# Smaller pieces in which spilled rows and the last matrix's weights are loaded, in a graph-convolution kernel

## The chip, the cores and the metric

One Trainium2 chip, one core of it. The metric is the device time of one launch in microseconds. A core has a matrix engine (TensorE, PE in the profile), a vector engine (VectorE, DVE), a scalar engine (ScalarE, ACT), GpSimd (POOL), a queue processor SP that issues DMAs, and 16 DMA engines that carry them.

## The reference

A graph of 6250 service nodes with 200,000 random edges goes through two graph convolutions of width 32. Then 512 requests, each a user and three services, are looked up, laid side by side (128 features) and multiplied by a 128 x 6250 matrix.

```python
def gcn_conv(x, W, b, src, dst, n):
    h = x @ W
    s, d = concatenate([src, arange(n)]), concatenate([dst, arange(n)])
    deg = segment_sum(ones, d, n);  dis = rsqrt(deg)
    msgs = h[s] * (dis[s] * dis[d])[:, None]
    return segment_sum(msgs, d, n) + b
g = relu(gcn_conv(service_emb, W1, b1, src, dst, 6250))
g = gcn_conv(g, W2, b2, src, dst, 6250)
x = concatenate([user_emb[user_idx], g[context_idx].reshape(512, 96)], axis=1)
return x @ fc_W + fc_b            # 512 x 6250, float32
```

## The kernel before

The sum over edges is made a dense product. The nodes are cut into 49 chunks of 128, and the 49 chunks of destinations into 14 groups (`SIZES`): one of 1 chunk, two of 2 chunks, eleven of 4. The adjacency of a group is a table of small counts in fp8, one 128 x 128 tile for each source chunk and destination chunk: 196 tiles for a group of four chunks, 25,088 bytes in each of the 128 partitions.

Up to about 330 us the edges are sorted. From there to 593 us the groups are built one after the other: TensorE makes the tiles out of one-hot rows (L1431), ScalarE evicts them into one of three slots, and TensorE at once uses them for the first layer (L1449, tile `psY`). Since three slots don't hold 14 groups, SP writes each of the first 11 to DRAM (`spill`, L573).

Then comes the second layer, in the order `ORDER`: the last three groups, which still lie in their slots, and then groups 10, 9, ... down to 0, which are read back. Five slots are in use now, `place2[i]` for the i-th group. Four programs run side by side:

- TensorE (from L1493) waits for `loaded` of the group's slot and runs 49 matmuls of 96 columns for each chunk, each with a weight load of its own (L1449, tile `pp`), then raises `y2_done`.
- SP (from L592) issues the reloads in the same order. The loads of the groups at places 3 and 4 wait only for TensorE's last tile of the building stage (`filled`); those at place i from 5 on wait for `y2_done` of i - 4, which says that group i - 5 has left the slot. After the reloads SP loads the last matrix (`load_fc`): its weights once `y2_done` is 10, its bias, spread over all partitions, once it is 11. Both count on `fc_in`.
- VectorE sums the three parts of a group (L1221) and scales them (L1223, L1213).
- ScalarE's queue writes the result to a table in DRAM (L803): 128 bytes for each node, 64 KB for a group of four chunks.

When all table rows are in DRAM, GpSimd gathers the requests' rows (L677), TensorE turns them into features (L1530, L1535), waits for all of `fc_in`, and multiplies by the last matrix in blocks of 512 columns (L1550). VectorE adds the bias, and the result leaves on the queues of SP and ScalarE.

The reload splits each group in four (`LOAD_PARTS`), so a DMA moves 6272, 3136 or 1600 bytes of each partition for a group of 4, 2 or 1 chunks. The last matrix goes in pieces of `FC_PART` = 1568 columns of four bytes; its weights take two DMAs a piece (96 and 32 partitions), its bias one.

Of the kernel before, what the change touches and what calls it, by code (L numbers as in the profile page):

```python
# [92 lines left out]
SPILL_PARTS = 4  # L93
RUN_UP = (8, 12, 36)
AHEAD_OF = {1: 12, 3: 6}
LOAD_PARTS = 4
FC_PART = 1568


UNIT = 2.0 ** -9  # L100
# [36 lines left out]
def chunks_of(g):  # L137
    return SIZES[g]


def first_chunk(g):
    return sum(SIZES[1:g]) if g else sum(SIZES[1:])
# [6 lines left out]
def group_of(b):  # L149
    return next((g for g in range(1, NG) if b < first_chunk(g) + SIZES[g]), 0)  # L150
# [13 lines left out]
def tiles_of(g):  # L164
    return NH * chunks_of(g)


def bytes_of(g):
    return -(-tiles_of(g) // 2) * 2 * P


def pairs_of(g):
    return -(-tiles_of(g) // PAIR)


def first_half(g):
# [23 lines left out]
def pairs_before(g):  # L200
    return sum(pairs_of(k) for k in range(g))


def gcn_kernel(nc, user_idx, context_idx, edge_index, user_emb, service_emb,
# [13 lines left out]
    with ctx:  # L218
        def sem(name):
            return ctx.enter_context(nc.semaphore(name))  # L220
# [72 lines left out]
        def at(offset, size, dt):  # L293
            return arena[:, offset:offset + size].bitcast(dt)
# [123 lines left out]
        loaded = [sem(f"loaded{k}") for k in range(5)]  # L418
# [73 lines left out]
        for k, counted_then in enumerate(tiles_by):  # L492
            needed = sum(c0 < counted_then for _, c0, _ in begun)
            assert units_ready(TURN_STAGES[k] - 1, k) >= UNITS * needed and words_ready_by(TURN_STAGES[k], k) >= WORDS * needed
# [6 lines left out]
        ORDER = list(range(NG - SLOTS, NG)) + list(range(NG - SLOTS - 1, -1, -1))  # L501
        KEPT = [g % SLOTS for g in ORDER[:SLOTS]] + [3, 4]
        place2 = [KEPT[i % 5] for i in range(NG)]
        NSPILL = NG - 3

        def adj_tile(slot, n):
            return adj8[slot][:, n // 2, :, n % 2]

# [19 lines left out]
        def _(sp):  # L528
# [39 lines left out]
            for g in range(NSPILL):  # L568
                for k in range(SPILL_PARTS):
                    a, b = (pairs_of(g) * n // SPILL_PARTS for n in (k, k + 1))  # L570
                    c, e = (min(n * PAIR // 2 * 2 * P, bytes_of(g)) for n in (a, b))
                    sp.wait_ge(evicted, pairs_before(g) + b)
                    sp.dma_start(spill[g, :, c:e], at(adj_at[g % SLOTS] + c, e - c, U8)).then_inc(spilled[g % SLOTS], 16)  # L573
# [5 lines left out]
            def load_fc(slot, what):  # L579
                tile = at(adj_at[slot], N * 4, F32)  # L580
                whole = fc_W if what == 0 else fc_b[None, :].to_broadcast((P, N))
                for c in range(0, N, FC_PART):
                    w = min(FC_PART, N - c)
                    if what == 0:
                        sp.dma_start(tile[0:CTX * D, c:c + w], whole[D:P, c:c + w]).then_inc(fc_in, 16)
                        sp.dma_start(tile[CTX * D:P, c:c + w], whole[0:D, c:c + w]).then_inc(fc_in, 16)
                    else:
                        sp.dma_start(tile[:, c:c + w], whole[:, c:c + w]).then_inc(fc_in, 16)

            with sp.If(is_bad == 0):  # L590
                sp.wait_ge(filled, pairs_before(NG))
                for i in range(3, NG):  # L592
                    if i >= 5:
                        sp.wait_ge(y2_done, i - 4)
                    part = -(-bytes_of(ORDER[i]) // LOAD_PARTS)
                    for c in range(0, LOAD_PARTS * part, part):
                        w = min(part, bytes_of(ORDER[i]) - c)
                        sp.dma_start(at(adj_at[place2[i]] + c, w, U8), spill[ORDER[i], :, c:c + w]).then_inc(loaded[place2[i]], 16)
                for k in range(2):
                    sp.wait_ge(y2_done, NG - 4 + k)  # L600
                    load_fc(place2[(NG + k) % 5], k)
# [79 lines left out]
        def _(act):  # L681
# [97 lines left out]
            for g in range(NG):  # L779
                if g >= SLOTS:  # L780
                    act.wait_ge(spilled[g % SLOTS], 16 * SPILL_PARTS * (g // SLOTS))
                    act.wait_ge(y_done, g - SLOTS + 1)
                if g == 2:
                    act.wait_ge(flags_set, 3)
                for k in range(pairs_of(g)):
                    gp = pairs_before(g) + k
                    n0, n1 = k * PAIR, min((k + 1) * PAIR, tiles_of(g))
                    m0, m1 = n0 // 2, -(-n1 // 2)
                    act.wait_ge(filled, gp + 1)
                    nc.scalar.mul(adj16[g % SLOTS][:, m0 * P:m1 * P], bank(gp)[:, 0:(m1 - m0) * P], PAIR_SCALE).then_inc(evicted, 1)  # L790
                    if g and k == LAG - 1:
                        set_y(g - 1)
                    if g + 2 < NG and k in relative_at(g):
                        relative(g + 2, relative_at(g).index(k))
# [24 lines left out]
        def _(dve):  # L819
# [184 lines left out]
            def on_stage(step, cur, stages, turns):  # L1004
                histogram(units_ready(stages, turns))
                if stages in GLUE_AT:
                    for part in GLUE_AT[stages]:
                        glue(part)
                _, level, bit, mirror, domain = step
                s, t = keys[cur], keys[1 - cur]  # L1010
                dve.wait_ge(sorted_to, stages + 1)
# [275 lines left out]
            def mix_features(b):  # L1287

                dve.wait_ge(feat_mixed, b + 1)
                V.tensor_scalar(featT[0:CTX * D, b * P:(b + 1) * P], psX[0:CTX * D, b % 2 * P:(b % 2 + 1) * P], bias2[:, 0:1], None, ALU.add).then_inc(feat_ready, 1)  # L1290
            copy_features(0)
            mix_features(0)
            dve.wait_ge(fc_in, 48 * -(-N // FC_PART))
            n = 0
# [15 lines left out]
        def _(pe):  # L1310
# [136 lines left out]
            def spread(tile, layer, slot, n, c):  # L1447
                b, dd = divmod(n, c)
                return MM(tile[:, dd * D3:(dd + 1) * D3], adj_tile(slot, n), features(layer, b), start=(n == 0), stop=(n == NH * c - 1))  # L1449
# [4 lines left out]
            def run_up(n, tile=pp[1][:, BANK:2 * BANK]):  # L1454

                for _ in range(n):
                    MM(tile[:, 0:P], ident[:], above[:], start=True, stop=True)
# [27 lines left out]
            g = NG - 1  # L1485
# [6 lines left out]
            with pe.If(is_bad == 0):  # L1492
                for i, g in enumerate(ORDER):  # L1493
                    c = chunks_of(g)
                    tile = pp[i % 3]
                    if i >= 3:
                        pe.wait_ge(y2_read, i - 2)
                        pe.wait_ge(loaded[place2[i]], 16 * LOAD_PARTS * (i // 5 + (1 if i % 5 >= 3 else 0)))
                    for b in range(NH):
                        if i == 0 and b == first_chunk(group_of(b)):  # L1500
                            pe.wait_ge(x_done, group_of(b) + 1)
                        for dd in range(c):
                            ins = spread(tile, 1, place2[i], b * c + dd, c)
                    ins.then_inc(y2_done, 1)
                run_up(RUN_UP[2])
# [26 lines left out]
            def weigh_features(b):  # L1532

                pe.wait_ge(feat_copied, b + 1)
                MM(psX[0:CTX * D, b % 2 * P:(b % 2 + 1) * P], W2b[:], featT[0:CTX * D, b * P:(b + 1) * P], start=True, stop=True).then_inc(feat_mixed, 1)  # L1535
            pe.wait_ge(users_in, 16 * BB)
            turn_features(0)
            weigh_features(0)
            pe.wait_ge(fc_in, 48 * -(-N // FC_PART))
            n = 0  # L1540
# [33 lines left out]
```

## Time and profile before

| | us |
|---|---|
| median of three runs | 767.07 (767.07 to 769.0) |
| the profiled execution | 769.29 |
| its span | 767.5 |

The span is measured between the first and the last instruction of the profiled execution; its own time contains the little that lies around it. In the profile, queue q1 is that of SP, q10 that of ScalarE, q0 that of GpSimd, and q8 carries instructions. The granted clock is a share of TensorE's full 2.4 GHz. "issue" in the chain of waits is time in which an engine waited for nothing that the profile shows. The share of a DMA queue is the time its packets took, as a share of 16 engines' time; it can pass 100% in a short stretch, as a packet is counted whole where it starts. A stretch can be asked for by itself; its rows are then those of packets and issues that start in it.

### The profile page before, as it was taken

What the parts mean: (1) busy time and instruction counts of PE and PEld (TensorE: products, weight loads), DVE (VectorE), ACT (ScalarE), POOL (GpSimd) and SP (SyncE); (2) the same over time, 40 slices, a digit from 0 to 9 for tenths busy, and PEclk for the clock granted to TensorE, in tenths of its full rate; (3) what the DMA queues carried; (4) which work ended last, traced back from release to release, by engine and by line L of the source; (5) the groups of instructions that cost most, each with busy time, mean ns of one, the idle gap of its engine ahead of it and who ended that gap; (6) DMA issues with size and microseconds to landing.
All of it is one profiled execution on the core that took longest, in us unless ns stands there. A gap on an engine that the chain in (4) does not pass through costs nothing.

```text
span 767.5 us, 21867 instructions
## 1 busy us (share of the span) xinstructions
PE 600.2 (78%) x9504; PEld 563.7 (73%) x9504; DVE 600.4 (78%) x1436; ACT 423.3 (55%) x770; POOL 178.6 (23%) x181
## 2 busy tenths in 40 slices
PE   0453657747657755578699999999999999998897
PEld 0343657747657854478699999999999999998543
DVE  9999999999999999786999999999982211111386
ACT  4996188889879311357588888888877000000000
POOL 1100000020000000577766666666100000000500
PEclk9967779799778875589899999999999999999999
DMA  7000000000000000245366665556000999859376
GB/s 128 2 1 1 1 1 1 1 5 2 1 4 1 2 0 1 72 112 177 120 204 210 210 200 196 193 207 210 13 3 23 417 415 399 286 132 274 90 306 284
DMA packets 39143, 94.13 MB, mean 123 GB/s; under 512 B 19097, under 2 KB 21843, under 8 KB 39044
## 3 DMA queue, kind: packets, MB, share of 16 engines
q1 hardware_dynamic: 24340, 74.28, 26.3%
q0 software_dynamic: 5216, 9.91, 6.0%
q10 hardware_dynamic: 9488, 8.52, 3.5%
q8 instruction: 76, 1.25, 0.7%
q14 instruction: 23, 0.19, 0.1%
HBM read 48.50 MB, written 44.18 MB: 121 GB/s over the span
## 4 chain that ended last, share of the span: by engine, by line
PE 52%; DVE 37%; issue 3%; ACT 3%; POOL 2%; DMA 2%; SPq 0%; DVEq 0%; POOLq 0%
PE pp L1431 17%; PE pp L1449 14%; PE psY L1449 13%; DVE arena L962 12%; DVE arena L963 12%; PE pp L1550 6%; DVE arena L949 3%; POOL arena L656 2%; ACT arena L713 2%; PE pp L1367 1%; DMA arena<-ordered_keys,window 1%; DVE arena L957 1%; DVE arena L958 1%; PE psX L1418 1%; DVE arena L960 1%
## 5 line engine op out<-in xcount | busy, mean ns | idle before, releaser
L656 POOL DMA_INDIRECT arena<-ordered_keys,window x147 | 157.3, 1070 | 217.9 <-DMA ordered_keys<-arena 147.5
L790 ACT ACTIVATE arena<-pp 128x512 uint16<-128x512 f32 x308 | 172.0, 584 | 43.5 <-PE pp L1431 41.2
L1431 PE MATMUL pp<-arena 128*128 128x128 fp8e4 (+1 forms) x2401 | 189.4, 221 | 7.7 <-DVE arena L1141 7.7
L713 ACT ACTIVATE arena<-arena,neg_word 128x780 fp8e4<-128x780 bf16 (+1 forms) x200 | 170.1, 945 | 0.0
L1431 PEld LDWEIGHTS pp<-arena 128*128 128x128 fp8e4 (+1 forms) x2401 | 148.3, 98 | 8.2 <-issue 6.2
L1449 PE MATMUL psY<-arena 128*128 128x96 bf16 x2401 | 150.6, 207 | 2.7 <-ACT y_s L774 2.6
L1449 PEld LDWEIGHTS psY<-arena 128*128 128x128 fp8e4 x2401 | 123.4, 98 | 2.9 <-ACT arena L790 2.7
L1140 DVE TENSOR_SCALAR arena<-arena 128x384 int32<-128x384 int32 (+5 forms) x224 | 111.0, 496 | 7.4 <-PE pp L1431 7.3
L1449 PE MATMUL pp<-arena 128*128 128x96 bf16 x2401 | 105.8, 207 | 8.2 <-issue 8.2
L1449 PEld LDWEIGHTS pp<-arena 128*128 128x128 fp8e4 x2401 | 104.3, 99 | 9.8 <-issue 9.7
L962 DVE TENSOR_TENSOR arena<-arena 128x832 f32<-128x832 f32 (+4 forms) x121 | 107.5, 888 | 3.9 <-ACT arena L736 1.1
L963 DVE TENSOR_TENSOR arena<-arena 128x832 f32<-128x832 f32 (+4 forms) x121 | 106.9, 884 | 0.0
L1347 PE MATMUL psY<-arena 128*128 128x128 fp8e4 x1024 | 74.7, 242 | 25.6 <-DVE arena L949 21.1
L1347 PEld LDWEIGHTS psY<-arena 128*128 128x128 fp8e4 x1024 | 74.1, 143 | 27.0 <-issue 14.4
L1367 PE MATMUL pp<-ident,arena 128*128 128x128 f32 x202 | 39.6, 373 | 57.2 <-DVE arena L963 57.1
L1221 DVE TENSOR_REDUCE arena<-pp 128x128 f32<-128x384 f32 (+2 forms) x14 | 7.1, 508 | 95.2 <-PE pp L1449 95.2
L1367 PEld LDWEIGHTS pp<-ident,arena 128*128 128x128 f32 x202 | 34.3, 197 | 59.8 <-DVE arena L963 59.8
L1141 DVE TENSOR_SCALAR arena<-arena 128x384 int32<-128x384 int32 (+5 forms) x224 | 73.1, 327 | 0.0
L766 ACT ACTIVATE arena<-arena,neg_low 128x128 f32<-128x128 f32 x147 | 47.9, 391 | 16.9 <-DMA arena<-ordered_keys,window 16.8
L677 POOL DMA_INDIRECT feat<-context_table,ccl x12 | 11.3, 943 | 174.8 <-DMA context_table<-arena 171.4
L1550 PE MATMUL pp<-arena 128*128 128x512 f32 (+1 forms) x104 | 44.8, 586 | 0.5 <-DVE arena L1290 0.5
L1347 PE MATMUL pp<-arena 128*128 128x128 fp8e4 x539 | 39.4, 242 | 6.5 <-ACT arena L713 6.5
(205 smaller groups left out, 518.8 us busy)
## 6 DMA issues: line engine op xcount, KB each, us to landing
arena<-adjacency_spill SPq DMA_DIRECT2D x32, 784.0 KB, 10.5
adjacency_spill<-arena SPq DMA_DIRECT2D x24, 768.0 KB, 4.0
adjacency_spill<-arena SPq DMA_DIRECT2D x8, 832.0 KB, 4.0
out_dram<-arena SPq DMA_DIRECT2D x12, 512.0 KB, 2.6
out_dram<-arena ACTq DMA_DIRECT2D x8, 512.0 KB, 2.9
arena<-adjacency_spill SPq DMA_DIRECT2D x8, 392.0 KB, 4.8
arena<-ordered_keys,window POOLq DMA_INDIRECT x147
arena<-in_L_rec_fc_b_dram SPq DMA_DIRECT2D x3, 784.0 KB, 12.2
```

Source lines behind the costliest of these rows:

```text
L656: nc.gpsimd.indirect_dma_start(gath[:, k, q, :], None, ordered, bass.IndirectOffsetOnAxis(ap=window[:, q, d:d + 1], axis=0)).then_inc(gat[ ...
L713: ins = nc.scalar.activation(cols8[n % BUFS][:, 4 * u:4 * u + 4, 0:c1 - c0], high4[:, :, c0:c1], ACT.Sign, bias=neg_word[:, u:u + 1], satu ...
L790: nc.scalar.mul(adj16[g % SLOTS][:, m0 * P:m1 * P], bank(gp)[:, 0:(m1 - m0) * P], PAIR_SCALE).then_inc(evicted, 1)
L962: V.tensor_tensor(o_low, low, high, ALU.min)
L963: return V.tensor_tensor(o_high, low, high, ALU.max)
L1140: V.tensor_scalar(src32[h][:, i, :, 0:b - a], bit32[:, 0:4, a:b].bitcast(I32), abs(BIT - i), BITS, shift, ALU.bitwise_and)
L1141: ins = V.tensor_scalar(dst32[h][:, i, :, 0:b - a], bit32[:, 4:8, a:b].bitcast(I32), abs(BIT - i), BITS, shift, ALU.bitwise_and)
L1347: ins = MM(counts_of(s), cols8[n % BUFS][:, :, i], rows8[n % BUFS][:, :, i, :], start=False, stop=False)
L1367: ins = nc.tensor.transpose(ps[q][:, b * P:(b + 1) * P], src[:, c + b * P:c + (b + 1) * P], ident[:])
L1431: ins = MM(bank(gp)[:, (n - n0) // 2 * P:((n - n0) // 2 + 1) * P], src_hot(h, n - a), dst_hot(h, n - a), start=n % 2 == 0, stop=n % 2 == 1 ...
L1449: return MM(tile[:, dd * D3:(dd + 1) * D3], adj_tile(slot, n), features(layer, b), start=(n == 0), stop=(n == NH * c - 1))
L1550: MM(bank(n)[:, 0:w], featT[:, b * P:(b + 1) * P], fcW[:, c:c + w], start=True, stop=True).then_inc(fc_mm, 1)
```

## The change

The number of pieces of a reload now goes with the group's chunks: `loads_of(g)` is 4 for each chunk, so 16, 8 or 4 DMAs for a group, of 1568 bytes a partition (1600 for the group of one chunk, whose 49 tiles are rounded up to 50). What TensorE waits for is counted by `loads_to`, which sums the loads that went to the slot so far. `FC_PART` goes from 1568 to 784 columns, so the weights take 16 DMAs and the bias 8.

```diff
-LOAD_PARTS = 4
-FC_PART = 1568
+LOADS_A_CHUNK = 4
+FC_PART = 784
...
+def loads_of(g):
+    return LOADS_A_CHUNK * chunks_of(g)
...
+        def loads_to(i):
+
+            return sum(loads_of(ORDER[k]) for k in range(3, i + 1) if k % 5 == i % 5)
...
-                    part = -(-bytes_of(ORDER[i]) // LOAD_PARTS)
-                    for c in range(0, LOAD_PARTS * part, part):
+                    part = -(-bytes_of(ORDER[i]) // loads_of(ORDER[i]))
+                    for c in range(0, loads_of(ORDER[i]) * part, part):
...
-                        pe.wait_ge(loaded[place2[i]], 16 * LOAD_PARTS * (i // 5 + (1 if i % 5 >= 3 else 0)))
+                        pe.wait_ge(loaded[place2[i]], 16 * loads_to(i))
```

SP's queue before, from the branch after the building stage (L590) on: the reloads (L598, partitions x bytes), the weights of the last matrix (L585 and L586, partitions x columns), and its bias (L588).

```order
L590 COMPARE_AND_BRANCH
L598 DMA arena<-adjacency_spill 128x6272 x32
L598 DMA arena<-adjacency_spill 128x3136 x8
L598 DMA arena<-adjacency_spill 128x1600 x4
L585 DMA arena<-in_L_rec_fc_W_dram 96x1568
L586 DMA arena<-in_L_rec_fc_W_dram 32x1568
```

The same place of SP's queue in the changed kernel, whose lines are 8 further down:

```order
L598 COMPARE_AND_BRANCH
L606 DMA arena<-adjacency_spill 128x1568 x144
L606 DMA arena<-adjacency_spill 128x1600 x4
L593 DMA arena<-in_L_rec_fc_W_dram 96x784
L594 DMA arena<-in_L_rec_fc_W_dram 32x784
```

44 reloads have become 148, with the last group's four as they were, and each pair of weight DMAs holds half the columns (there are eight pairs now, and were four). No instruction has moved past another on any engine.

## Rows read from the trace of the kernel before

**Rows 1.** The page of the kernel before, its header.

```profile
span 767.5 us, 21867 instructions
```

**Rows 2.** Chain that ended last, 592.2 to 720 us: start us, length us, what.

```profile
593.46 0.32 issue
...
606.65 0.61 issue
607.26 5.60 PE pp L1449 x128
612.86 0.60 issue
...
672.53 0.61 issue
673.14 21.88 PE pp L1449 x511
695.02 2.42 issue
697.44 7.17 PE pp L1449 x127
704.62 0.21 issue
...
708.34 2.62 DMA context_table<-arena
...
718.49 2.16 PE pp L1550 x3
```

**Rows 3.** Waits, 590 to 720 us: total us, times, longest us.

```profile
PE pp L1449 <- issue: 8.2, 13, 2.4
```

**Rows 4.** DMA, 597 to 657: queues (packets, MB, share); issues (KB, us to landing).

```profile
q1 hardware_dynamic: 4317, 24.08, 97.6%
...
q8 instruction: 10, 0.16, 1.0%
...
context_table<-arena ACTq DMA_DIRECT2D x6, 64.0 KB, 12.0
```

**Rows 5.** DMA, 610.9 to 611.0 us.

```profile
q8 instruction: 1, 0.02, 61.2%
```

**Rows 6.** DMA, 670.7 to 670.9 us.

```profile
q8 instruction: 1, 0.02, 29.6%
```

**Rows 7.** DMA, 674.2 to 674.4 us.

```profile
q8 instruction: 1, 0.02, 31.7%
```

**Rows 8.** DMA, 680.0 to 680.2 us.

```profile
q8 instruction: 1, 0.02, 28.8%
```

**Rows 9.** DMA, 694.4 to 694.6 us.

```profile
q8 instruction: 1, 0.02, 43.9%
```

**Rows 10.** Windows: stretch, PE, PEld, DVE, ACT, POOL busy; then granted clock, DMA share, GB/s.

```profile
698.80:702.20 3.40, 3.40 (x48) 3.40 (x44) 0.81 (x3) 0.00 (x0) 0.00 (x0) 0.50 1.04 339
```

**Rows 11.** DMA, 677.4 to 678.4 us.

```profile
q1 hardware_dynamic: 247, 0.35, 97.6%
```

**Rows 12.** DMA, 675.8 to 682 us.

```profile
q1 hardware_dynamic: 572, 0.81, 45.1%
...
context_table<-arena ACTq DMA_DIRECT2D x1, 64.0 KB, 5.7
```

**Rows 13.** Timeline of SP's queue, 592 to 600 us: start us, us, what.

```profile
592.30 4.21 SPq L598 DMA_DIRECT2D arena<-adjacency_spill  x8
```

**Rows 14.** Timeline of SP's queue, from 684 us.

```profile
684.21 0.35 SPq L585 DMA_DIRECT2D arena<-in_L_rec_fc_W_dram  x1
...
692.54 1.77 SPq L588 DMA_DIRECT2D arena<-in_L_rec_fc_b_dram  x4
```

**Rows 15.** DMA, whole span: the last piece of the bias.

```profile
arena<-in_L_rec_fc_b_dram SPq DMA_DIRECT2D x1, 773.0 KB, 16.6
```

**Rows 16.** DMA, 667.1 to 670.7 us, an issue of this stretch.

```profile
context_table<-arena ACTq DMA_DIRECT2D x1, 64.0 KB, 6.8
```

## The prediction

> **What bounds the kernel now.** I read the page's header first [rows 1]: the execution spans 767.5 us; its own time is 769.29, the median of three runs 767.07. The change touches only loads that SP issues after 592 us, so next I read the chain that ended last from there [rows 2]. From 593.8 to 707.5 us it is TensorE's second layer, one matmul row after another, cut by pieces called "issue": 0.61 us at 606.65, then one behind nearly every 128 matmuls (that is 256 instructions, each matmul has its weight load), 0.61 at 672.53, then 2.42 at 695.02 and 0.21 at 704.62. The waits by engine add all of them to 8.2 us in 13 stops [rows 3]. The stops come by count of instructions and not at a group's start (196 matmuls), where TensorE would wait for a load: no load is late.
>
> The DMA view says what they are. From 597 to 657 us SP's queue keeps the 16 engines busy for 97.6% of the time, and beside it q8 carries 10 packets of instructions of about 16 KB each (0.16 MB), as many as TensorE uses blocks of 256 instructions [rows 4]. The block that began at 607.26 had its successor's packet start at 610.9, 3.6 us later [rows 2, 5]; TensorE ran dry at 612.86 and went on at 613.46, 2.5 us after that start. So a packet that starts within 5.60 - 2.5 = 3.1 us of the block costs nothing, and a later one costs the excess. Four more starts: 3.8 us after the block that began at 672.53 - 5.60 = 666.93, under pieces of 3136 bytes [rows 6]; 1.1 us after 673.14, with the engines idle [rows 7]; 1.4 us after 673.14 + 5.47 = 678.61 (5.47 is a quarter of the four blocks in 21.88), under pieces of 1600 bytes [rows 8]; 4.9 us after 673.14 + 3 x 5.47 = 689.55, under the weights of the last matrix [rows 9]. The start at 4.9 us made the 2.42 us stop, and behind it the granted clock was 0.50 (the 1.2 GHz level) for 3.4 us [rows 10]: the next 128 matmuls took 7.17 us and not 5.60 [rows 2].
>
> **The change, part by part.** The reload goes from 44 DMAs to 8 x 16 + 2 x 8 + 4 = 148; rows of 6272 or 3136 bytes become 1568 (1600 in the last group). The last matrix takes 16 DMAs and its bias 8, where they took 8 and 4, with rows of 3136 bytes. Same bytes, same gates, same order.
>
> *Stops under the reload.* They are 8.2 - 0.32 (the branch at 593.46) - 2.42 - 0.21 = 5.25 us. What stands in front of an instruction packet? Over the idle start of 1.1 us the 6272-byte stretch adds 2.5 us. A packet there takes 0.245 us on an engine (24.08 MB in 0.976 x 16 x 60 us is 25.7 bytes a ns), so about 10 packets. If the number of packets in front is what stays, 10 to 16 of them at 0.07 us add 0.7 to 1.1 us: the start is at 1.8 to 2.2 us, under 3.1, and all 5.25 us go. If the bytes in front stay (10 x 6272 = 63 KB, 40 small packets, 2.8 us), the start is at 3.9 and the stops stay. For the first speaks rows 8, 1.4 us under nearly the pieces that the change wants; against it that this load was only four DMAs long and nearly drained, and rows 6, where pieces of half the size gained nothing (3.8 us). I take 5.25 gone, zero as the other end.
> The Trainium skill ("DMA: Bandwidth & Descriptors", section "Queues, rings and completion order") says that an engine drains a whole packet, typically 9 to 17 descriptors, from one queue before it turns to the next. The 10 worked out for 6272 bytes agree with it, the 3136-byte start does not (2.7 us of packets half as long would be some 20); by it the stops go, by a count of bytes they would stay.
>
> *Stops under the last matrix.* 2.42 + 0.21 us of stop and 7.17 - 5.60 = 1.57 us of slow clock: 4.2 us. The packets there become half as long, not a quarter, and rows 6 show 3136 bytes still late. Bounds 0 and 4.2; I take half, 2.1 us.
>
> *Are the loads still in time?* A group of 4 chunks is needed every 196 x 43.75 ns = 8.6 us (5.60 us for 128). In the best microsecond of the 1600-byte load 0.35 MB moved at 97.6% [rows 11], 22.4 bytes a ns, 70 ns for 1568 bytes; over the whole short load 0.81 MB at 45.1% of 6.2 us [rows 12] gives 18.1 bytes a ns, 87 ns. All reloads are 148 x 8 = 1184 packets for each engine, plus some 5 us of table rows and semaphores. From 592.8 at 70 ns they end at 681; the group that is needed last of the full ones, the eighth, is there by 668 and wanted at 593.8 + 10 x 8.6 = 679.5. SP issued its first eight in 4.21 us, 0.53 each [rows 13]: 16 take 8.4 us, inside 8.6. It is late by the first two groups' 32 issues (17 us against a gate at 602), and hardly catches up, but slots are loaded some 20 us ahead. I take the cost as 0; the cover is this lead.
>
> *The last matrix's loads.* Issued at 684.21, bias at 692.54 [rows 14], its last piece landing 16.6 us after its issue [rows 15], the last of four in 1.77 us and so at 693.9: at 710.5: 26.3 us in all. TensorE wants them at 718.49 [rows 2], 8.0 us later. Now the gate opens 5.25 us earlier (679) and the need comes 7.35 - 2.4 = 4.95 us earlier (713.5). With 681 as start of the data and 1 us for shorter rows they land near 707: hidden, 6 us spare.
>
> *The last table write, late instead.* It took 2.62 us, its queue just drained [rows 2]. TensorE now ends at 700, while the bias loads run to 706, and a write beside them is slow: 12.0 us for 64 KB beside 6272-byte packets [rows 4], 6.8 beside 3136 [rows 16], 5.7 beside 1600 [rows 12]. For this last one of 16 KB beside 3136-byte packets I bound 2.6 and 6.8 us and take 5.0: 2.4 us lost (0 to 4.2). The gather and the features wait for it.
>
> Sum: -5.25 - 2.1 + 2.4 = -4.95 us. The profiled execution would come to 764.3; set on the median, 767.07 - 4.95 = **762.1 us**. Own range: 759.0 to 765.5.
>
> **The rivals.**
> *Bytes in front, not packets.* The stops stay at 0.4 to 0.8 us. Since the smaller packets keep the engines full to 681 and not 672, one or two more blocks (at 673 and 678) meet a stop: +1. Time 767.5 (766 to 769). For it: rows 6. Against it: rows 8.
> *The loads become the bound (the other side).* Its place is the reload. The last matrix's data must begin by 713.5 - 25.3 = 688 to be in time; 1184 packets and 5 us must fit in 95 us, so it decides from 76 ns a packet, or 0.65 us for an issue of SP. At 87 ns [rows 12] the eighth full group ends at 592.8 + 8 x (128 x 0.087 + 0.4) = 685 against 679.5, and all reloads at 701; weights and bias follow to 726, features wait for them and not for the table, and the time is 718.5 to about 726: +7, 774 us. Against it: the 87 ns contain the slow first packets and the tail of a four-DMA load, and rows 11 show 70; in its favour, nothing here shows a long stretch of such packets, and 76 lies between.
> The Trainium skill (same page, section "Bandwidth") asks for DMAs of at least 1 MiB, with about 2.0 us of fixed cost each. Taken one behind the other, 148 DMAs of 200 KB at an estimated 2.46 us would be 364 us. The trace denies that they go one behind the other: four of 200 KB were all down in 6.2 us at most [rows 12].
> *Everything gains.* All stops and the slow clock go, 9.4 us, and the table write loses 0 to 2 because the weights, too, run ahead: 758.5. For it: 1.57 us hang on one stop alone. Against it: rows 6.
>
> **How the numbers follow.** Forecast 0.46; bytes in front 0.20; loads the bound 0.20; everything gains 0.10; mixtures, 0.04. A change of 0.3% (2.3 us) is what a measurement can tell. Faster: 0.46 x 0.95 + 0.10 + a tenth of the second and third = 0.58; the second rival gives most of the 0.20 for the same, the third most of the 0.22 for slower. Range 757.5 to 772.5: it leaves out about 0.15 of the slow case and 0.03 below.
>
> **What would show it.** In the chain of the changed kernel: no "issue" every 128 matmuls between 594 and 680; TensorE's 1965 matmuls there unbroken and the gate of the last matrix at about 679. q8's packets start within 3 us of a block. The reload's last packet near 681 (at 688 or later the slow rival begins). The last table write 5 us long. One stop of about 1 us between 680 and 700, and perhaps no stretch at 0.50 clock. It is wrong if stops stay at 0.6 us, or if a stop stands at the start of a group and not by count: that would be a late load.

## The result and the profile after

The changed kernel takes 763.0 us in the median of 20 runs (759.55 to 769.0), the kernel before 767.07 (761.98 to 770.12, 20 runs). The ratio is 0.9954, 95% interval 0.9937 to 0.9972: 0.5% faster, 4.1 us between the medians. Single runs of either kernel spread over 8 to 10 us, so the traces below are compared from the second layer's own entry, its first matmul.

The header and the chain that ended last of the changed kernel, from 585 us (start us, length us, what); both answers, since the long piece hides where the layer begins:

```profile
span 758.4 us, 21983 instructions
```

```profile
590.61 0.30 issue
590.91 3.10 PE pp L1457 x69
```

```profile
591.97 98.64 PE pp L1457 x2321
690.61 1.76 issue
692.37 2.68 PE pp L1457 x59
...
695.89 4.17 DMA context_table<-arena
...
703.38 3.21 DMA feat<-context_table,ccl
...
708.82 9.43 PE pp L1558 x16
```

Its waits from 590 to 720 us (total us, times, longest us), to be held against [rows 3]:

```profile
PE pp L1457 <- issue: 2.1, 2, 1.8
```

The stops under the reload (ten of 0.33 to 0.82 us in the kernel before, 5.25 us in all) are gone; of [rows 2] only the branch and one stop of 1.76 us under the last matrix's weights are left, and no slow clock follows it in this trace. Windows of the layer (stretch, PE, PEld, DVE, ACT, POOL busy, granted clock, DMA share, GB/s):

```profile
590.90:674.40 83.50, 83.49 (x1965) 83.50 (x1966) 13.30 (x37) 0.22 (x1) 0.00 (x0) 1.00 1.04 356
674.40:684.10 9.70, 9.70 (x233) 9.70 (x230) 2.28 (x6) 0.00 (x0) 0.00 (x0) 1.00 1.05 287
684.10:692.40 8.30, 6.54 (x155) 6.43 (x152) 0.81 (x3) 0.00 (x0) 0.00 (x0) 1.00 1.05 294
```

The DMA view of 597 to 657 us answers to [rows 4] (queue: packets, MB, share of 16 engines; issues: KB, us to landing):

```profile
q1 hardware_dynamic: 15129, 21.09, 99.1%
...
q8 instruction: 11, 0.18, 1.1%
...
arena<-adjacency_spill SPq DMA_DIRECT2D x106, 196.0 KB, 4.0
context_table<-arena ACTq DMA_DIRECT2D x7, 64.0 KB, 5.3
```

The reload moves 21.1 MB where it moved 24.1, at full engines, and a table write beside it lands in 5.3 us and not 12.0. A reload DMA lands 4.0 us after its issue. SP issues without a pause (timeline of its queue from 591 us, start and length in us; the first three of the 148 reload DMAs were issued before, from 589.45 us on):

```profile
590.76 83.21 SPq L606 DMA_DIRECT2D arena<-adjacency_spill  x145
674.40 0.35 SPq L593 DMA_DIRECT2D arena<-in_L_rec_fc_W_dram  x1
```

That is 0.574 us for each 200 KB, or 350 GB/s, about what the engines move: the load queue never gets long. The bytes of all DMAs issued so far, less those of the packets begun, are what stands in the queue. Counted so every six microseconds from 596 to 674 us, 25 to 45 rows an engine are waiting (40 to 70 KB); in the kernel before, from 596 to 656 us, they swung between 7 and 47 rows of 6272 bytes (45 to 296 KB).

The two kernels from the layer's first matmul (us after it). Each row is one profiled execution, and the changed kernel's two are 3.5 us apart at the end, so differences of 2 to 3 us mean little:

| kernel | entry at | layer ends | table landed | last matrix starts | span ends |
|---|---|---|---|---|---|
| before | 593.8 | 113.7 | 117.2 | 124.7 | 173.7 |
| changed | 590.9 | 104.1 | 109.2 | 117.9 | 167.5 |
| changed, again | 597.3 | 106.0 | 109.2 | 116.7 | 164.0 |

Of the 9.1 us between the first two spans, 2.9 are the entry, which the change doesn't touch; 9.6 are gained in the layer, 2.8 given back between layer and last matrix, 0.6 in the last matrix. In the second trace of the changed kernel the layer gains 7.7. Its stop under the weights is followed by a slow clock, as in the kernel before (59 matmuls in 4.25 us and not 2.68; granted clock 0.60 from 699.0 to 703.3 us, so mostly the 1.2 GHz level):

```profile
696.97 2.04 issue
699.01 4.25 PE pp L1457 x59
```

The last matrix differs only in its first 16 matmuls, by the clock: 8.80 us before (granted 0.81), 9.43 in the first trace (0.75), 7.10 in the second (1.00). TensorE had waited 1.2, 3.6 and 0.9 us for the gathered features just before.

### The profile page after: what moved, and what is told of

It reads as the page before. It is cut to its first block, busy times and chain, and to the rows that moved or that the text cites. A ratio compares the mean times of both kernels' runs of the same rounds, so it can differ in the third digit from the quotient of the medians.

```text
span 758.4 us, 21983 instructions
## 1 busy us (share of the span) xinstructions
PE 591.7 (78%) x9504; PEld 555.6 (73%) x9504; DVE 600.8 (79%) x1436; ACT 423.1 (56%) x770; POOL 179.4 (24%) x181
## 4 chain that ended last, share of the span: by engine, by line
PE 53%; DVE 37%; ACT 3%; issue 2%; POOL 2%; DMA 2%; SPq 0%; DVEq 0%; POOLq 0%
PE pp L1439 17%; PE pp L1457 13%; PE psY L1457 13%; DVE arena L970 13%; DVE arena L971 12%; PE pp L1558 6%; DVE arena L957 3%; POOL arena L664 2%; ACT arena L721 2%; PE pp L1375 1%; DVE arena L965 1%; DMA arena<-ordered_keys,window 1%; DVE arena L966 1%; PE psX L1426 1%; DVE arena L968 1%
## 5 line engine op out<-in xcount | busy, mean ns | idle before, releaser
L1457 PE MATMUL pp<-arena 128*128 128x96 bf16 x2401 | 102.4, 206 | 2.1 <-issue 2.1
L1457 PEld LDWEIGHTS pp<-arena 128*128 128x128 fp8e4 x2401 | 102.1, 98 | 2.3 <-issue 2.3
L1355 PEld LDWEIGHTS psY<-arena 128*128 128x128 fp8e4 x1024 | 73.9, 143 | 26.1 <-issue 13.8
L1314 DVE TENSOR_TENSOR arena<-pp,arena 128x512 f32<-128x512 f32 (+1 forms) x52 | 33.9, 658 | 11.2 <-PE pp L1558 10.6
```

What stands on the lines that cost most here:

```text
L1355: ins = MM(counts_of(s), cols8[n % BUFS][:, :, i], rows8[n % BUFS][:, :, i, :], start=False, stop=False)
```

## The experiments

In three of them the last matrix is as before (1568 columns), in the others as in the changed kernel, unless said. Ratios are to the kernel before, timed on the same chip.

**The reload alone.**

```diff
-FC_PART = 784
+FC_PART = 1568
```

> The reload in 1568-byte rows, the last matrix in pieces of 1568 columns as before. If the packets in front of an instruction packet count (theory P), the ten stops of 0.3 to 0.8 us under the reload go (5 us) and the stop of about 2.4 us with its slow clock under the weights stays: second layer about 108 us long instead of 113.7, time 1 to 4 us under before. If the whole gain came from the last matrix's pieces, this run equals before.

Ratio 0.9939 (0.9909 to 0.997). Its chain:

```profile
593.73 94.31 PE pp L1457 x2215
688.04 1.92 issue
689.96 5.57 PE pp L1457 x127
695.53 2.63 issue
698.16 4.23 PE pp L1457 x59
...
703.22 2.39 DMA context_table<-arena
```

The layer is 108.7 us long, as expected, and the whole measured gain is here, though it ends 4.6 us later than the changed kernel's first trace: by its end no load is waiting in the queue any more, and the table write is short.

**The last matrix alone.**

```diff
-    return LOADS_A_CHUNK * chunks_of(g)
+    return LOADS_A_CHUNK
```

> The reload in four pieces a group as before, the last matrix in pieces of 784 columns. Theory P: about ten stops under the reload, 5 us, stay; the stop under the weights falls from 2.4 to 1 to 2 us without a slow clock. Second layer about 111 to 112 us, time 0 to 3 us under before. If the last table write loses 1.5 to 3 us beside the shorter rows, that eats it: no change.

Ratio 1.0006 (0.9982 to 1.003), no change. Stops under the reload 0.23 to 0.61 us each, nine of them, one of 1.66 under the weights and no slow clock: the layer ends after 109.1 us, 4.6 before the old one, but the last matrix starts only 3.7 earlier and the span ends 2.7 earlier in this trace (its first 16 matmuls take 9.85 us, at a granted clock of 0.72); the median shows none of it.

**Wide rows in small DMAs.**

```diff
-                        sp.dma_start(at(adj_at[place2[i]] + c, w, U8), spill[ORDER[i], :, c:c + w])...
+                        for p in range(0, P, 32):
+                            sp.dma_start(at(adj_at[place2[i]] + c, w, U8)[p:p + 32, :], spill[ORDER[i], p:p + 32, c:c + w])...
```

> As many and as large DMAs as the changed kernel (148 of 200 KB), but each of 32 partitions with rows of 6272 bytes (6400 in the last group), two packets an engine. Theory P (what stands in front are packets, each as long as its row): rows of 6272 bytes bring the stops of 0.4 to 0.8 us back, 4 to 6 us in all, although the DMAs are small. Rival D (small DMAs let the instruction packets through): no stops under the reload, as in the changed kernel.

Ratio 1.0511 (1.0462 to 1.056). Stops came back, and far larger. Chain, and the reload in the DMA view of 597 to 657 us:

```profile
605.79 2.86 issue
608.65 6.94 PE pp L1458 x128
615.59 1.73 issue
617.32 5.60 PE pp L1458 x128
622.92 3.07 issue
```

```profile
q1 hardware_dynamic: 3417, 14.30, 98.7%
...
arena<-adjacency_spill SPq DMA_DIRECT2D x92, 196.0 KB, 21.3
```

The instruction packet of the block at 617.32 starts at 623.1, 5.8 us in. So small DMAs alone don't let the instruction packets through. It isn't clean, though: DMAs of 32 partitions also move only 14.3 MB in the 60 us, 15 bytes a ns and engine, which alone makes anything in front of an instruction packet last longer. SP, which issues faster than that, has 150 to 336 KB an engine waiting from 608 us on.

**Rows of 3136 bytes.**

```diff
-LOADS_A_CHUNK = 4
+LOADS_A_CHUNK = 2
```

> Rows of 3136 bytes throughout the reload (2 DMAs a chunk). Theory P with 10 to 16 packets in front at 0.124 to 0.142 us: instruction packets start 2.3 to 3.4 us into a block: no stops or a few under 0.3 us, under 1 us in all. Rival B (a fixed number of bytes in front): starts at 3.6 us or later and ten stops, 4 to 5 us in all; but B already fails on the changed kernel's starts at 0.8 to 2.4 us, so a threshold in the row's length between 1568 and 3136 would be its last refuge.

Ratio 1.0029 (1.0005 to 1.0054). Ten stops of 0.33 to 0.60 us under the reload. Packets are half as long, and the instruction packets start where they did. This was the first sign against the prediction's count of packets. In the block that begins at 605.72 the packet comes 3.5 us in (DMA view, 609.2 to 609.4 us):

```profile
q8 instruction: 1, 0.02, 27.5%
```

**Rows of 12544 bytes.**

```diff
-    return LOADS_A_CHUNK * chunks_of(g)
+    return 2
```

> Two DMAs a group, rows of 12544 bytes, the last matrix in pieces of 784 columns. Theory C, formed from the runs so far: an instruction packet waits for what already stands in the load queue of its engine, but for no more than some 90 KB of it, whatever the rows' length. It expects starts 3.5 to 4 us into a block, stops of 0.3 to 0.9 us, as with rows of 6272 bytes. Theory P, the prediction's (some 10 to 16 rows in front, each as long as its bytes): 10 rows of 0.47 us, starts 5 us or more into a block and stops of 2 us and more.

One execution, 768.23 us. Nine stops of 0.17 to 0.72 us under the reload: no worse than at 6272 bytes. A packet here lasts 0.48 us; ten of them would have made stops of nearly 3 us. In the block that begins at 607.13 the instruction packet starts 3.5 us in.

**Short rows, deep queue.** The decisive one: the rows of the changed kernel in the DMAs of the old one.

```diff
+                    part = bytes_of(g) // (4 * n)
+                    to = at(adj_at[place2[i]], bytes_of(g), U8).rearrange("p (n k w) -> p k n w", k=4, w=part)
+                    of = spill[g, :, 0:bytes_of(g)].rearrange("p (n k w) -> p k n w", k=4, w=part)
+                    for k in range(4):
+                        sp.dma_start(to[:, k], of[:, k]).then_inc(loaded[place2[i]], 16)
```

> Rows of 1568 bytes as in the changed kernel, but four of them from each partition in one DMA: 44 DMAs of up to 784 KB as before, so SP runs ahead and the queue is as deep in bytes as before. The last matrix in pieces of 1568 columns. Theory C: with 90 KB in front of an instruction packet (57 rows, 3.8 us) the stops of 0.3 to 0.8 us come back although the rows are short. Theory P (10 to 35 rows in front): starts at 1 to 2.5 us, no stops under the reload, second layer as with the 1568-byte reload alone (108.7 us).

Ratio 1.0018 (0.9994 to 1.0043): no gain left. Its waits from 590 to 720 us, its chain, the DMA view of 611.1 to 611.2 us, and that of 597 to 657 us:

```profile
PE pp L1459 <- issue: 9.5, 14, 2.4
```

```profile
607.27 0.30 issue
607.58 5.60 PE pp L1459 x128
613.18 0.33 issue
...
619.11 0.60 issue
```

```profile
q8 instruction: 1, 0.02, 59.7%
```

```profile
q1 hardware_dynamic: 14787, 22.48, 101.5%
...
arena<-adjacency_spill SPq DMA_DIRECT2D x28, 784.0 KB, 11.7
```

As many packets of the load queue as in the changed kernel (14787 against 15129), but a DMA lands 11.7 us after its issue and not 4.0, the instruction packet starts 3.5 us into its block, and the stops are all back. So short rows alone don't free the instruction packets, and a count of packets in front doesn't describe them: the same rows without the long queue (the reload alone) had no stop.

Put together, a start less the idle start of 1.1 us [rows 7], times the engines' rate, is an estimate of what was in front: 2.5 us at 25.7 bytes a ns are 64 KB with rows of 6272; 2.4 at 24.8 are 60 KB with 3136; 2.4 at 26.0 are 62 KB with 12544; 2.4 at 23.1 are 55 KB here; and 4.7 at 15.1 are 71 KB in the wide rows of small DMAs. In packets the same are 10, 19, 5, 35 and 11. Nor is it one DMA of the load queue: one holds 50, 25, 100, 50 and 12.5 KB an engine. The idle start isn't always the same (0.4 us after 684.02 us in the kernel before), so these are good to some 20 KB.

Counted over all traces, TensorE's blocks split by what stood in the load queue when they began. In each of the 46 blocks with 100 KB or more an engine (DMAs over 128 partitions, rows of 1568 to 12544 bytes) the instruction packet started 3.4 to 3.9 us in, and a stop followed. With 60 to 75 KB it started 1.0 to 2.5 us in under rows of 1568 and 1600 bytes (21 blocks), and 2.5 to 4.0 us in under longer ones (10 blocks). A short queue and short rows go together in the changed kernel; how much the rows add when the queue is short, no run here separates.

**Wide rows, paced.**

```diff
+                        if len(sent) >= DEPTH:      # DEPTH = 2
+                            sp.wait_ge(sent[-DEPTH], 16 * sent.count(sent[-DEPTH]))
```

> DMAs and rows of before (6272 bytes, last matrix in pieces of 1568 columns), but SP issues a reload only when the one before the last has landed: at most two are out, 16 rows an engine. Theory C: the queue in front is mostly one DMA or less (8 rows, 2 us) and never the full 16 for long: starts at 1.5 to 3.2 us, at most a few stops under 0.3 us. Theory P: rows of 6272 bytes, at least 8 to 10 in front as long as the engines are busy: stops stay. The loads themselves come a little later, never late for a group.

Ratio 1.0269 (1.0228 to 1.031). In the timeline of TensorE the first 1066 matmuls run unbroken, where the old kernel had six stops. Then three stops by count of instructions come back (0.25, 0.44 and 0.63 us), and from 654 us on the loads are late (waits, 590 to 722 us):

```profile
593.99 45.47 PE L1464 MATMUL pp<-arena 128*128 128x96 bf16 x1066 [0.29 <-issue]
639.71 5.57 PE L1464 MATMUL pp<-arena 128*128 128x96 bf16 x127 [0.25 <-issue]
645.72 5.60 PE L1464 MATMUL pp<-arena 128*128 128x96 bf16 x128 [0.44 <-issue]
```

```profile
PE pp L1464 <- DMA arena<-adjacency_spill: 15.0, 5, 4.5
```

A DMA lands 6.3 us after its issue, so two at a time move 1.6 MB in 6.3 us, 255 GB/s. The expectation "never late" was wrong. In the six blocks from 601.3 to 633.9 us, at whose start 21 to 60 KB an engine were waiting, the instruction packets started 0.8 to 2.5 us in; in the three blocks after them, with 52 to 73 KB, 3.5 to 3.9 us in. The load queue kept the engines busy only 82% of the time from 600 to 640 us, so not everything here was as before but the queue. That a shorter queue alone cures wide rows is made likely by the first six blocks and not shown.

**Rows of 784 bytes.**

```diff
-LOADS_A_CHUNK = 4
+LOADS_A_CHUNK = 8
```

> The changed kernel with the reload in rows of 784 bytes: 296 reload DMAs of 100 KB. If an issue of SP costs 0.48 to 0.57 us whatever its size, the reload takes 142 to 169 us and is the bound from the sixth group on: a group of four chunks comes every 15.4 to 18 us, the second layer ends 45 to 75 us later, 805 to 840 us. No stop by instruction packets. If issuing were cheaper for small DMAs, the time would stay near that of the changed kernel.

One execution, 827.49 us. SP's timeline and the waits of 590 to 780 us:

```profile
591.53 149.26 SPq L606 DMA_DIRECT2D arena<-adjacency_spill  x277
```

```profile
PE pp L1457 <- DMA arena<-adjacency_spill: 46.3, 8, 7.1
```

An issue takes 0.54 us for 100 KB and 0.574 for 200, so half the bytes save SP next to nothing: the slow rival, at the next step down.

**Rows of 1568 bytes for the last matrix too.**

```diff
-FC_PART = 784
+FC_PART = 392
```

> The changed kernel with the last matrix in pieces of 392 columns (rows of 1568 bytes, 32 weight DMAs and 16 bias DMAs). Under C, SP issues a pair of weight DMAs (200 KB) in 0.9 us, slower than the engines move it, so the queue stays short: the stop of 1.8 us goes, second layer about 102.5 us, the last table write 3 us at most. Loads end near 703 after issuing takes 23 to 26 us, needed at about 706. Time 1 to 3 us under the changed kernel, ratio to before about 0.992. If the issues take over 0.6 us each, the loads are late for the features and it is slower than the changed kernel.

Ratio 0.9949 (0.9925 to 0.9973), no more than the changed kernel. The layer has no stop and takes 102.2 us, but SP is behind, and the chain ends in the bias:

```profile
707.06 6.65 DMA arena<-in_L_rec_fc_b_dram
...
713.75 8.52 PE pp L1558 x16
```

**A shared slot, and the changed kernel again.** The groups of two chunks share a slot, so the weights' gate opens a group earlier:

```diff
+        TURN = list(range(NG - 2)) + [NG - 3, NG - 2]
+        place2 = [KEPT[t % 5] for t in TURN]
...
-                    sp.wait_ge(y2_done, NG - 4 + k)
+                    sp.wait_ge(y2_done, NG - 5 + k)
...
+                step = FC_PART if what else FC_PART // 2
```

> The changed kernel with two moves more. The two groups of two chunks share one slot, so the weights of the last matrix may be loaded one group earlier (y2_done 9 and 10); and the weights come in pieces of 392 columns (rows of 1568 bytes, 32 DMAs), the bias in pieces of 784. Theory C: the queue is short while the weights load, so the stop of 1.8 us goes (second layer 103 us); SP, the slower side, is done at about 700 and the loads land by 703, before the features (709), so the last table write is 2.6 to 3 us: 2 to 5 us under the changed kernel, ratio to before 0.989 to 0.993. Rival (the tail is set by the drained queue whatever TensorE does): equal to the changed kernel.

> The changed kernel as it is, on the same chip as the shared slot, for a direct comparison: 0.993 to 0.997 of before, one stop of 1 to 2 us at the weights, a last table write of 3 to 5 us.

Shared slot 0.9954 (0.993 to 0.9977), changed kernel beside it 0.994 (0.9918 to 0.9962): no better. Its chain:

```profile
590.78 102.22 PE pp L1461 x2401
...
693.84 7.31 DMA context_table<-arena
```

The layer is free of stops, 2 to 4 us shorter than the changed kernel's, and all of it goes to the table write, 7.31 us beside the bias loads (50 KB an engine waited when it began, 138 KB three us later). The gate gave nothing, as SP comes from the reload at 674 us anyway.

**The bias left out.** This kernel leaves out the load of the last matrix's bias; VectorE adds what lies in the slot, so the result is not the reference's.

```diff
-                for k in range(2):
-                    sp.wait_ge(y2_done, NG - 4 + k)
-                    load_fc(place2[(NG + k) % 5], k)
+                sp.wait_ge(y2_done, NG - 4)
+                load_fc(place2[NG % 5], 0)
```

> The changed kernel without the 3.2 MB load of the last matrix's bias (VectorE adds what lies in the slot), so this run leaves the bias out. It asks how much of the tail hangs on the load queue being full when TensorE ends. Theory Q (the tail is set by the draining queue): the last table write falls from 4.2 to 2.4 us, the gather from 3.2 to 2.4, table landed 106 us after the layer's entry where the changed kernel has 109: 2 to 4 us under the changed kernel, ratio to before about 0.990. If the tail hung on TensorE alone, only the stop of 1.8 us could change, and the time by under 1 us.

Ratio 0.9857 (0.9803 to 0.9911). That is 6 to 7 us under the changed kernel by the ratios, 3.8 by the medians on one chip (758.39 and 762.16), over few runs; 2 to 4 were expected. Chain:

```profile
593.93 94.31 PE pp L1455 x2215
688.24 0.57 issue
...
697.74 2.38 DMA context_table<-arena
```

The table is down 106.2 us after the entry, as expected, and not 109.2; 1.1 us of that is the shorter stop under the weights. After it the gather takes 2.41 us where the changed kernel's first trace has 3.21, and the first 16 matmuls of the last matrix 7.10 where it has 9.43. So the tail of the changed kernel does hang on how full the load queue is when TensorE ends.

## Why the prediction was right

**The sum.** 762.1 us was forecast and 763.0 measured.
- *Stops under the reload, 5.25 us:* right in size, for another reason than the one given (below). All went.
- *Stops under the last matrix, 2.1 of 4.2 us:* in the first trace 1.76 us of 4.2 stay, so 2.4 went; in the second 2.04 and 1.57 of slow clock stay, so 0.6 went. The run with the last matrix alone shows no gain in the median, and in its trace the way from the layer's end to the span's end is 1.9 us longer than before.
- *Loads in time, 0:* right. TensorE waited for none. The reload was expected to end near 681; SP had issued the last but a few by 674.
- *The last table write, 2.4 us lost:* it took 4.17 us, 1.6 more than before, and 2.40 in the second trace of the same kernel, whose TensorE was 1.9 us slower. Both had it down at 109.2, which fits that whichever of TensorE and the queue is later sets it. What was missing is the same cost one step on: the gather took 3.21 us where it took 2.40 before, and the last matrix starts 13.8 us after the layer's end, where it was 11.0.
- *The layer as a whole:* it gained 9.6 us in the first trace and not 7.4 (7.7 in the second). Of the difference 0.3 is the second term, and 1.9 lie in the blocks themselves: 128 matmuls take 5.45 us when nothing stops them (102.22 us for 2401 in the shared slot's run) and took 5.60 between stops. A stop thus costs 0.15 us more than its "issue" says.

**The mechanism was wrong.** The step that failed is "If the number of packets in front is what stays". Behind a long queue it is rather the bytes that stay, an estimated 55 to 64 KB in 5 to 35 packets at full rate: that is the first rival's mechanism, and with the rows alone made short (short rows, deep queue) the stops stayed, as that rival said. But the change did a second thing, which neither reckoned with: SP needs 0.574 us to issue 200 KB and the engines no longer, so the queue doesn't grow. The rival's 3.9 us took for granted that 63 KB in front mean the same delay in any queue. In the changed kernel 44 to 69 KB an engine were waiting at the start of the 16 blocks from 598 to 685 us, and their instruction packets started 0.7 to 2.3 us in (the block starts counted back from 692.37 by 256 instructions each). Less 1.1 us, that is the time of 27 KB or 17 rows at most, less than was waiting. So the 5.25 us came out by luck as far as the mechanism goes: the predicted starts of 1.8 to 2.2 us were near the measured ones, for a reason that the prediction didn't have.

The start of 3.8 us under shorter rows [rows 6] was read as the weaker evidence and was the stronger; the early one [rows 8] was early since that load had nearly drained, which the text said and then overrode. The rule of the Trainium skill ("DMA: Bandwidth & Descriptors", section "Queues, rings and completion order"), 9 to 17 descriptors drained before another queue's turn, agreed with the 10 of the 6272-byte rows. No run here bears it out as the cause of this delay: by the same estimate 5 packets stood in front at 12544 bytes, 35 at 1568.

**The slow rival** was to decide from 76 ns a packet or 0.65 us an issue. In the trace after, 21.09 MB in 0.991 of 16 x 60 us are 22.2 bytes a ns, 71 ns for 1568 bytes, and an issue takes 0.574 us: its 87 ns were too slow, and it still stood only some 10% away. The step to 784 bytes shows SP's issue as the first limit, 60 us slower. The fixed cost of 2.0 us a DMA, which the prediction takes from the Trainium skill ("DMA: Bandwidth & Descriptors"), stands there in the section "Anatomy of one DMA — SWDGE (gpsimd) path", for DMAs that GpSimd issues; no run here shows it for those of SP.

What stays open: why some 60 KB go first behind a long queue and less than is waiting behind a short one, what the length of the rows adds there, and how the 4.1 us of the medians divide, since the changed kernel's two traces differ by 6.4 us in the part before the layer and by 3.5 us after its entry.

## What to carry to other kernels

A stop that came by count of instructions and not at a data hand-over was instruction fetch here; look for its packets in the DMA view, and at what the load queues hold when they start. These loads, with some 20 us of lead, gained nothing from being issued early and in bulk: an issuer that was no faster than the engines kept the queue short, and the instruction packets and the table writes got through. Before shortening rows for such a reason, vary the rows and the length of the queue separately, as the deep-queue run does. When it has worked, look at what the same queue does to the next small transfer on the path: there part of the gain was lost.

## What the runs showed of the hardware that was not expected

- With 100 KB or more an engine in the load queue, an instruction packet started 3.4 to 3.9 us into its block in 46 of 46 blocks, with rows of 1568, 3136, 6272 and 12544 bytes: an estimated 55 to 64 KB go first, be they 5 rows or 35.
- An issue of SP takes 0.43 us for 128 rows, and 0.9 to 1.9 us about once in each TensorE block, at the time an instruction packet moves (changed kernel, 15 of 148). One of 128 x 4 rows took 0.5 to 0.7 us with up to 94 rows an engine waiting and 1.1 to 3.2 us from 99 on (deep-queue run); that run's average of 1.93 (40 in 77.07 us) contains these and SP's waits for a free slot.
- DMAs over 32 partitions with rows of 6272 bytes moved 245 GB/s in all, those over 128 partitions with the same rows 410.
- A stop of TensorE costs 0.15 us more than the "issue" that the chain shows for it: 5.60 us for 128 matmuls between stops, 5.45 without them.
